# A cross-attention and mixture-of-experts block on one core: the first attention's mask moved to TensorE, its banks and small steps regrouped

## What is computed

```
x = x + attention0(layernorm(x), ctx, ctx, mask)     # one head, 16 batches
x = x + moe_encoder(layernorm(x), ...)               # 4 experts, 2 per batch by a gate
x = x + attention1(layernorm(x), ctx, ctx, ...)      # 16 heads, causal
x = x + moe_ffn(layernorm(x), ...)                   # 8 experts, gathered tokens

attention0: scores = q @ k.T * 0.25; scores = where(mask == 0, -1e10, scores)
            softmax(scores) * KEEP @ v               # mask: one row of 128 flags a batch
gate:       layernorm(x).mean(tokens) @ gate_w.T + gate_b, then top 2 and softmax
```

## Time and profile before

| | us |
|---|---|
| median of 3 runs (860.32 to 863.5) | 860.49 |
| the profiled execution's own time | 862.72 |
| its span | 860.7 |
| first attention with the gate's choice, until ACT's first copy of a block | 0 to 111.62 |
| PE busy over the span | 729.6 (85%) |
| DVE, POOL, ACT busy over the span | 636.4, 387.1, 344.0 |

### The profile page before, as it was taken

The page is one execution under the profiler, slowest core; times in us unless marked ns, Lnnn a source line. Parts: engine busy times, 40 slices in busy tenths (PEclk is TensorE's granted clock), DMA queues, the critical chain, the costliest instruction groups (busy, mean ns, idle before and its releaser), DMA issues.

```text
span 860.7 us, 29825 instructions
## 1 busy us (share of the span) xinstructions
PE 729.6 (85%) x10940; PEld 580.7 (67%) x10941; DVE 636.4 (74%) x1925; ACT 344.0 (40%) x702; POOL 387.1 (45%) x664
## 2 busy tenths in 40 slices
PE   4688559999999999999999999998988898744885
PEld 3577547877877787878887788885665565422663
DVE  3786655777777777777777777788999999845865
ACT  4554324443434444343434344343454445321210
POOL 2899713344435353444434454443434454335132
PEclk9755578999999999999999999999999999965797
DMA  8877300000000000000000000001222212112000
GB/s 305 271 228 221 105 2 3 3 3 2 0 0 0 0 0 0 0 0 0 0 0 0 0 1 3 9 14 61 85 78 76 85 57 80 55 54 92 14 1 6
DMA packets 24722, 41.21 MB, mean 48 GB/s; under 512 B 3612, under 2 KB 16678, under 8 KB 24408
## 3 DMA queue, kind: packets, MB, share of 16 engines
q1 hardware_dynamic: 23960, 38.70, 13.8%
q0 software_dynamic: 704, 1.71, 0.7%
HBM read 31.88 MB, written 8.91 MB: 47 GB/s over the span
## 4 chain that ended last, share of the span: by engine, by line
PE 71%; DVE 15%; issue 6%; ACT 4%; POOL 2%; DMA 2%; SPq 0%; POOLq 0%; DVEq 0%
PE ps L453 8%; PE ps L459 7%; PE ps L461 6%; PE ps L460 6%; PE ps L639 6%; PE ps L621 5%; DVE mx L1377 4%; PE ps L571 4%; PE ps L677 4%; PE ps L679 3%; PE ps L678 3%; PE ps L573 3%; PE ps L572 3%; PE ps L563 2%; PE ps L675 2%
## 5 line engine op out<-in xcount | busy, mean ns | idle before, releaser
L1783 POOL TENSOR_TENSOR rs<-mv,cst 128x1 f32<-128x1 f32 x132 | 28.9, 219 | 343.3 <-DVE mv L1149 306.2
L1377 DVE TENSOR_REDUCE mx<-ps 128x16 f32<-128x2048 f32 x48 | 109.8, 2287 | 1.6 <-PE ps L594 1.6
L1005 ACT ACTIVATE pT<-ps 128x1024 f32<-128x1024 f32 x96 | 93.0, 1021 | 31.5 <-PE ps L621 29.4
L677 PE MATMUL ps<-xh,w_hi 128*128 128x128 bf16 x512 | 100.1, 220 | 0.0
L679 PE MATMUL ps<-xh,w_lo 128*128 128x128 bf16 x512 | 100.0, 219 | 0.0
L678 PE MATMUL ps<-xl,w_hi 128*128 128x128 bf16 x512 | 99.9, 219 | 0.0
L1785 POOL TENSOR_TENSOR rs<-rs,cst 128x1 f32<-128x1 f32 x132 | 74.2, 562 | 10.3
L459 PE MATMUL ps<-w_hi,hh 128*128 x256 | 70.1, 274 | 0.0
L460 PE MATMUL ps<-w_hi,hl 128*128 x256 | 69.8, 273 | 0.0
L461 PE MATMUL ps<-w_lo,hh 128*128 x256 | 69.8, 273 | 0.0
L1810 POOL TENSOR_TENSOR w_lo<-stage,w_hi 128x384 bf16<-128x384 f32 x64 | 58.8, 945 | 8.3 <-ACT w_hi L927 8.3
(11 more groups left out here) (355 smaller groups left out, 2518.1 us busy)
## 6 DMA issues: line engine op xcount, KB each, us to landing
stage<-in_w SPq DMA_DIRECT2D x32, 384.0 KB, 3.9
vec<-in_vec SPq DMA_DIRECT2D x4, 896.0 KB, 5.2
vec<-in_tw SPq DMA_DIRECT2D x12, 256.0 KB, 2.8
ctxc<-in_ctx SPq DMA_DIRECT2D x19, 128.0 KB, 2.1
comb<-x SPq DMA_DIRECT2D x16, 128.0 KB, 1.7
comb<-t SPq DMA_DIRECT2D x16, 128.0 KB, 1.8
shared<-x1b SPq DMA_DIRECT2D x16, 128.0 KB, 1.7
out<-x SPq DMA_DIRECT2D x16, 128.0 KB, 1.8
```

The source lines that it names most:

```text
L677: mm(dst, w(w_hi, c, j), xh[:, c, :], start=False, stop=False)
L1005: A(pT[:, 8 * a:8 * a + 8, :].rearrange("p h q -> p (h q)"), ps[:, 2 * a:2 * a + 2, :].rearrange("p g k -> p (g k)"), ACT.Exp, scale=SCALE ...
L1377: nc.vector.tensor_reduce(mx[:, :], att.rearrange("p g s k -> p (g s) k"), AX.X, ALU.max, negate=True).then_inc(m_max, 1)
```

## The change

The mask is no longer brought to all 128 partitions (1 MB) but as one row of 8 KB and as a column array of flags. Masked keys become zero by TensorE: the context is multiplied by a diagonal matrix of the flags (`diag`, made by ACT in `mask_diagonals`) in the place of its transposition, and the large negative constant enters the scores as a product of a row of ones with the row `neg`. DVE's mask steps go; the maximum, its negation, the sum's reciprocal and its factor are made for both batches in one instruction. The exponential reads PSUM. Scores, transposed probabilities and values take banks by the parity of the pair. The gate's weights are centred once (`gate_centred`), so its sums need no product with the mean. PE's, ACT's and DVE's orders are rewritten; six of the first DMAs are issued by ACT; the four transfers of bias rows come one pair later, the last after the loop; POOL waits for `g_ready` before it splits the causal weights, and the waits for `vec_in` stand before the blocks.

```diff
             def both_transposed(i):
...
                     transposed(lambda c: ya[j][:, 128 * c:128 * c + 128], 4 * j, 0, KC)
-                    transposed(lambda c: ctx[j][:, 128 * c:128 * c + 128], 4 * j, 256, KC).then_inc(a_T, 1)
+                    pe.wait_ge(a_split, n[j])
+                    for c in range(KC):
+                        last = mm(ps[:, 4 * j, D + 128 * c:D + 128 * c + 128], ctx[j][:, 128 * c:128 * c + 128], diag[j],
+                                  start=True, stop=True)
+                    last.then_inc(a_T, 1)
...
+                    mm(dst, ones[0:1, :], neg[:, (i * 2 + j) * S:(i * 2 + j + 1) * S], start=True, stop=False)
                     for c in range(KC):
-                        last = mm(ps[:, 4 * j + 1, 0:128], yca[j][:, 128 * c:128 * c + 128],
-                                  yca[j][:, D + 128 * c:D + 128 * c + 128], start=(c == 0), stop=(c == KC - 1))
+                        last = mm(dst, yca[j][:, 128 * c:128 * c + 128],
+                                  yca[j][:, D + 128 * c:D + 128 * c + 128], start=False, stop=(c == KC - 1))
...
-                    mm(dst[:, KC:KC + 1], mv[:, slot + j, 0:1].broadcast_to([128, 128]), rs[:, slot + j, :],
-                       start=True, stop=True).then_inc(a_gm, 1)
...
             for i in range(PAIRS):
                 if i + 1 < PAIRS:
                     both_transposed(i + 1)
+                if i == 0:
+                    pe.wait_ge(gw_in, 32)
+                    for c in range(KC):
+                        last = mm(ps[:, 7, 0:E], ones[:, :], gw[:, c, :], start=(c == 0), stop=(c == KC - 1))
+                    last.then_inc(g_sums, 16)
+                probs_transposed(i)
+                if i + 1 < PAIRS:
                     pair_scores(i + 1)
-                probs_transposed(i)
...
+            mask_diagonals(0)
             both_evict(0)
+            mask_diagonals(1)
             for i in range(PAIRS):
+                pair_exps(i)
                 if i + 1 < PAIRS:
                     both_evict(i + 1)
+                probs_evict(i)
+                if i + 2 < PAIRS:
+                    mask_diagonals(i + 2)
                 weights_high(i, 0)
-                pair_exps(i)
                 weights_high(i, 1)
-                probs_evict(i)
...
             for i in range(PAIRS):
-                if i >= 3:
-                    gate_means(i - 3)
                 if i + 1 < PAIRS:
                     pair_tokens(i + 1)
                 pair_maxima(i)
+                if i == 0:
+                    gate_centred()
                 if i > 0:
                     pair_x(i - 1)
+                if i >= 3:
+                    gate_means(i - 3)
...
                 weights_low(i, 3)
+            pool.wait_ge(g_ready, 1)
             pool.wait_ge(wc_hi_ready, 1)
...
-            pool.wait_ge(g_ready, 1)
+            pool.wait_ge(vec_in, 16 * E)
             pool.wait_ge(vc_in, 16)
```

More of the change, by code:

```diff
@@ L944, in pair_exps, with mask_diagonals @@
                     act.wait_ge(a_bias, i * 2 + (j + 1))
-                    A(ta[j][:, 0:128], ta[j][:, 128:256], ACT.Exp, bias=mx[:, 8 * j + 1:8 * j + 2], scale=SCALE_A,
-                      accum_out=mx[:, 8 * j + 2:8 * j + 3]).then_inc(a_p, 1)
+                    A(ta[j][:, 0:128], ps[:, 1 + 4 * (i % 2), 128 * j:128 * j + 128], ACT.Exp, bias=mx[:, 2 + j:3 + j], scale=SCALE_A,
+                      accum_out=mx[:, 4 + j:5 + j]).then_inc(a_p, 1)
+            def mask_diagonals(i):
+                if i == 0:
+                    act.wait_ge(mask_ready, 16)
+                for j in range(2):
+                    b = i * 2 + j
+                    A(diag[j], ident, ACT.Copy, scale=m01[:, b:b + 1]).then_inc(a_split, 1)
             def probs_evict(i):
-                for j in range(2):
-                    act.wait_ge(a_pT, i * 2 + (j + 1))
-                    copy(h[:, 512 + 128 * j:640 + 128 * j], ps[:, 4 * j + 2, 0:128]).then_inc(a_pTs, 1)
+                act.wait_ge(a_pT, i * 2 + 2)
+                copy(h[:, 512:768], ps[:, 2 + 4 * (i % 2), 0:256]).then_inc(a_pTs, 2)
+            mask_diagonals(0)
             both_evict(0)
+            mask_diagonals(1)
             for i in range(PAIRS):
+                pair_exps(i)
                 if i + 1 < PAIRS:
                     both_evict(i + 1)
+                probs_evict(i)
+                if i + 2 < PAIRS:
+                    mask_diagonals(i + 2)
                 weights_high(i, 0)
-                pair_exps(i)
                 weights_high(i, 1)
-                probs_evict(i)
                 weights_high(i, 2)
@@ L1233, in gate_means, with gate_centred @@
             def gate_means(i):
-                for j in range(2):
-                    dve.wait_ge(a_gm, i * 2 + (j + 1))
-                    dst = gate_ps(i, j)
-                    ts(gmean[:, :, i * 2 + j:i * 2 + j + 1], dst[:, 0:KC].rearrange("p (c o) -> p c o", o=1),
-                       dst[:, KC:KC + 1], 1.0 / S, ALU.subtract, ALU.mult).then_inc(a_gmean, 1)
+                dve.wait_ge(a_gm, i * 2 + 2)
+                cp(gmean[:, :, i * 2:i * 2 + 2].rearrange("p c b -> p b c"), gate_ps(i)).then_inc(a_gmean, 2)
+            def gate_centred():
+                dve.wait_ge(g_sums, 16)
+                for c in range(KC):
+                    last = stt(gw[:, c, :], ps[:, 7, 0:E], -1.0 / D, gw[:, c, :], ALU.mult, ALU.add)
+                last.then_inc(g_centred, 16)
+            dve.wait_ge(maskt_in, 16)
+            ts(m01[:, :], maskt_i[:, :], 0.0, None, ALU.not_equal).then_inc(mask_ready, 16)
+            dve.wait_ge(x_in0, 16)
             pair_stats(0)
```

130 lines of the change are left out of this document (62 added, 68 removed).

## The result

The changed kernel takes 866.98 us, the median of 20 executions (860.94 to 870.09), against 861.26 of 20 of the kernel before (859.71 to 863.5): a ratio of 1.0057, 95% interval 1.0043 to 1.0072. The medians differ by 5.7 us, and the changed kernel is the slower one; the forecast was 859.5. Its profiled execution took 870.09 us with a span of 868.1, 7.4 us more than the 862.72 of before, and I split these 7.4 first: 2.4 lie ahead of ACT's first block copy, and 5.0 arise behind it, where the prediction expected nothing.

A forecast was written before the change was run, and what follows sets the result against it. A loop through POOL, DVE, TensorE and ACT, 10.5 us a pair, would replace TensorE's own order as the bound. Start +0.1, five pairs +2.3, last pairs -2.4, chain -2.0, wait +1.0 give -1.0: 859.5 us, range 854.5 to 864.0.

The forecast's parts named there:

- the price of the diagonals: ACT's two diagonals a pair, ahead of the cast: 0.20 us each, 0.40 for both, kept between 0.2 and 0.8.
- What bounds it: Attention pairs: a closed loop through POOL, DVE, TensorE and ACT takes over from TensorE's own order; TensorE 9.2, POOL 9.3.
- The circle's size: Attention pairs, from one POOL first quarter to the next: seven terms sum to 10.5 us a pair, between 10.3 and 10.9.
- The contended tokens: DVE's two token steps each wait out one POOL instruction: 1.91 us for two, against 0.73 with POOL silent.
- nothing else is as long: Attention pairs: no other limit reaches the loop's 10.5 us a pair; TensorE needs 9.2, POOL 9.3.
- The start: Up to POOL's first quarter: 9.3 + 6.3 + 2.6 = 18.2 us, against 17.37 before; the second pair's at 28.7.
- the path now has: Additions ahead of POOL's first quarter: longer transposition 0.85, gate weight sums 1.0, probabilities and diagonals 0.7, together 2.6 us.
- Last pairs and chain: From pair 6 to ACT's first block copy: last pairs -2.4 us, gate's chain -2.0, wait +1.0.
- The wait on POOL: POOL holds its causal split until the gate's choice: choice 2.0 us earlier, wait for POOL +1.0, copy at 110.6.
- What follows is the same program in both kernels.: Behind ACT's first block copy, at 111.62 us before: same program, so only arrival times at that copy were compared.
- Rival (3): ACT makes a longer loop, 11.3 to 11.6 us a pair: 863.5 to 865, chance 0.13.
- Rival (2): TensorE's clock rises to 2.4 GHz, shortening pairs, last sums and start: 855.6 to 857, chance 0.12.

The follow-up runs named there:

- c3: Kernel before with 17 one-row, one-column products and two already met waits, making TensorE's program 4416 bytes longer, as in the changed kernel: 862.59 us.
- a9: Changed kernel with 46 one-row, one-column products and some met waits, making TensorE's program 16384 bytes longer than before: 865.35 us, ratio 1.0040.
- after: The changed kernel itself, nothing edited, with its first profiled execution of 870.09 us: median 866.98 us.
- a3: Changed kernel with ACT's cast of a pair's first quarter put ahead of that pair's exponentials, pairs 1 to 7: 858.86 us, ratio 0.9971 to before.
- a7: Changed kernel with pair 0's four casts ahead of the first exponentials and POOL's roots of pair 2 behind pair 0's last quarter: 863.83 us.
- a11: Changed kernel with pair 0's casts first, POOL's roots of pair 2 later, and TensorE's program padded to 685504 bytes: 862.06 us, ratio 1.0005.
- a10: Changed kernel with casts ahead, altered start, bias rows in pair 6, gate weight sums behind pair 0's values, TensorE's program padded to 685504 bytes: 855.52 us, ratio 0.9946.
- a4: Changed kernel with ACT's two diagonals of pair i+2 behind the cast of pair i's first quarter: 861.69 us, ratio 1.0002 to before.

## Why the prediction was wrong

Four steps failed: the path of the start (2.3 us too short), the price of the diagonals and the subtractions that were left out (1.6 together over five pairs), and the statement that nothing changes behind the first block. The forecast had ACT's first copy 1.0 us earlier than before; it came 2.4 later, 3.4 behind the forecast. The steps in their order, with the profiled execution of the changed kernel:

- **What bounds it.** Right: the circle through POOL, DVE, TensorE and ACT, POOL waiting 1.6 us a pair for the cast (1.2 forecast). Shown by the cast ahead: 9.04 a pair.
- **The circle's size.** Forecast 10.5. The terms as measured, from 41.86: quarters 3.48, to the tokens 1.06, to the second copy 3.91, copy 0.48, probabilities 0.26, diagonals 0.60, cast and hand-over 0.90, together 10.69. One term was mis-sized: the diagonals, taken at 0.20 each between bounds of 0.1 and 0.4 and measured at 0.30. The exponential's row would have been the nearer one: a diagonal lasts 0.41 and 0.40, as the exponentials of the earlier trace rows do (0.40), and the profile lists both as ACTIVATE. The contended tokens (1.91) and the order of copies were right.
- **Missed interference.** The step that says that nothing else is as long left out DVE's four subtractions of the bias rows beside POOL's quarters, +1.2 us in one pair. The prediction had used this mechanism for the tokens and not asked which other DVE steps meet POOL once the pairs shift. The Trainium skill (SBUF — State Buffer, "Who interferes with whom") says that a DVE instruction with two inputs in SBUF contends with a GpSimd one that reads SBUF; the trace agrees, 4.75 for 3.52 us, also with 5 partitions. Five pairs took 54.06 against 52.5, and not more because the last took 10.11: the body of pair 6 writes no diagonals, since there is no pair 8, and the cast begins 0.27 behind the copy of the probabilities instead of 0.86. The prediction had charged them in all five.
- **The start.** Forecast 18.2, measured 20.50 (17.0 to 20.5 in the copies). The step "the path now has" counted one longer transposition, though TensorE does those of pairs 0 and 1 in a row (0.85 more), and left out that the scores of pair 0 stand between them, now with two rows of constants (1.46 for both). The row's price was also outside its bounds: 0.43 a batch at most by analogy, 0.73 measured here. This is the error ahead of the copy that costs most, for it makes the start hang on TensorE's clock: where TensorE was fast the first quarter came at 17.0 to 17.3, ahead of the forecast, and where it was slow at 19.3 to 20.5. That the executions differ there was not foreseen at all. The statistics at 9.6 instead of 9.3 were right.
- **Last pairs and chain.** From pair 6's first quarter every term is within 0.4: pair 7's at 93.2 (8.0 later; 8.1 forecast), the last sums 10.2 behind it (10.6), the choice 5.3 behind those (5.4), ACT's copy 5.25 behind the choice (5.3). The wait on POOL gained 1.1 in the changed kernel and 1.2 in the one before; the sum had 1.0.
- **The sum** at ACT's copy: 2.3 + 0.2 + 1.6 - 0.7 = 3.4 above the forecast's 110.6, 114.0.
- **"What follows is the same program in both kernels."** This first step failed too. It is the same program at another place of TensorE's instruction stream. Shown by c3 and a9 is that the place alone turns the times of single blocks in one kernel into those of the other: 0.3 to 0.4 us longer from block 29 to 31, 0.2 shorter from 5 to 6, and nothing over all blocks. Not shown is that the place makes the stall of 1.0 us with its 3.6. The stall stands in two traces (after and a3) out of ten with the changed place and in none of seven with the other, and in both a transfer of instructions was late. Four slow executions of c3, and the missing slowest ones of a9, fit a stall that comes with the place; the medians don't decide it.

Of the 5.7 us between the medians, the altered start with the padding took 4.9. The start's part is clear: 3.2 alone (a7) and 3.3 beside the padding (a11 against a9). The padding's part is not: 1.6 in a9, 1.8 from a7 to a11, 1.0 the other way in c3, 0.4 the wrong way in a10, and in a9 to a11 the faster TensorE of the start comes with it. The circle weighs as much as the start: the diagonals behind the cast took 5.3 of the 5.7 by themselves (a4), so these shares don't add up. What stays open is why a stall comes in one execution and not in the next, and why unprofiled executions lie above the profiled one in many of the changed kind (865.35 against 861.18 in a9, whose first four took 861.2 to 863.9 and whose other eight 865.3 to 866.7) and not in those of before. They leave no trace; a slow start and a fall at block 47 would make such a difference, 3 and 1.6 us, but that is argued and not shown.

Rival (3), the dearer ACT, had the right sign and the right engine for the diagonals only (0.30 where it has 0.39); the wide maxima were not in the way, and the tokens met POOL once (1.91). Its 863.5 to 865 is 2 us short of the median. Rival (2) was half right: the clock was higher in the pairs (0.68), and bought little since the circle hardly hangs on it.

## What to carry to other kernels

When an edit removes a wait of one engine, draw the next closed circle, and open it where the order of one engine closes it: here one cast moved ahead of two exponentials was worth 8 us by the medians (6.8 at the first maxima), more than the change itself moved. List every instruction of a DVE and POOL pair that will meet after the shift, however few partitions it has. Moving an interference to a stage where the same engine is the bound gains nothing, as the bias rows in pair 6 show. Added work at a place where an engine runs without pause is paid twice, in its time and in the spread that the clock gives it. And where the length of TensorE's program has changed, single blocks behind the edit differ by 0.2 to 0.4 us without any other reason.

## What was not expected of the hardware

TensorE's program is brought in during the run, in pieces of 16384 bytes: the traces have 40 such transfers for the 669120 bytes before and 41 for the 673536 after, and 41 in c3, where nothing but TensorE's program was lengthened. With 4416 bytes of filler blocks 29 to 31 go from 27.12 to 27.44, and with exactly one piece more than before they go back to 27.11. In the two traces where one piece came 6 to 8 us later than in the others, TensorE stood still for 1.00 and 0.94 us behind it.

A product of one row and one column in float32 takes TensorE 0.05 to 0.06 us (46 of them 2.44, 17 of them 0.99), so its program can be shifted almost for nothing. And the row of constants, one partition loaded, is not cheaper than a full product at the slow level but dearer, 0.73 against 0.43 us.
